# A folded layer's constant bias term: its own product replaced by two columns behind batch 1's x2

## The reference, cut to what matters

```python
x = x + L0(x, cond)      # base matrix + LoRA, summed over 8 experts
x = x + L1(x, cond)      # shared MLP + the 2 best of 8 experts' MLPs, 128 -> 512 -> 128
x = x + L2(x, cond)      # one expert of 8 (argmax of cond):
    # hidden = silu(x @ wu.T + bu) * (x @ wg.T + bg); out = hidden @ wd.T + bd
x = x + L3(x, cond)      # out = x @ (sum_g cond_g * weight_g * mask).T + bias
```

## Time and profile before

| | us |
|---|---|
| median of 3 runs | 72.28 |
| lowest and highest of them | 72.18, 72.62 |
| the profiled execution's own time | 72.77 |
| its span, first to last instruction | 71.5 |

### The profile page before, as it was taken

One profiled execution on the slowest core, in us unless ns is written; L12 is line 12 of the kernel. 1 busy time (PEld: TensorE's weight loads), 2 busy tenths in 40 slices (PEclk: granted clock), 3 DMA queues, 4 the chain that ended last, 5 costly groups with the idle time before them and its releaser, 6 DMA issues.

```text
span 71.5 us, 1059 instructions
## 1 busy us (share of the span) xinstructions
PE 68.1 (95%) x313; PEld 54.9 (77%) x313; DVE 45.2 (63%) x83; ACT 48.6 (68%) x97; POOL 36.7 (51%) x51
## 2 busy tenths in 40 slices
PE   5999999999999999999999999999999999999950
PEld 5976868778778778788788788787788788788640
DVE  0355669567655557765556775555986576958960
ACT  5225799466787666678766668869678895674660
POOL 5000478054999999866999986655540700000000
PEclk9999999999999999999999999999999999999998
DMA  0998799999500000000000000000000000000017
GB/s 3 240 339 286 288 392 375 409 413 416 218 5 9 0 0 0 0 0 0 0 5 5 0 0 0 0 0 9 0 0 0 0 0 0 0 0 0 0 40 253
DMA packets 2308, 6.62 MB, mean 93 GB/s; under 512 B 256, under 2 KB 768, under 8 KB 2304
## 3 DMA queue, kind: packets, MB, share of 16 engines
q1 hardware_dynamic: 2160, 6.44, 24.6%
q10 hardware_dynamic: 144, 0.13, 0.5%
HBM read 6.04 MB, written 0.52 MB: 92 GB/s over the span
## 4 chain that ended last, share of the span: by engine, by line
PE 95%; DVE 1%; issue 0%; DVEq 0%
PE gp L456 9%; PE gp L453 9%; PE gp L452 9%; PE acc L456 9%; PE acc L453 9%; PE acc L452 9%; PE up L456 9%; PE up L452 9%; PE up L453 9%; PE up L249 4%; PE acc L448 2%; PE acc L481 1%; PE up L607 1%; PE gp L448 1%; PE gp L438 1%; PE gp L568 1%
## 5 line engine op out<-in xcount | busy, mean ns | idle before, releaser
L379 ACT ACTIVATE act<-gp 128x512 f32<-128x512 f32 x24 | 14.3, 598 | 12.0 <-PE gp L456 11.5
L289 POOL TENSOR_TENSOR wlo<-raw_skill,whi 128x384 fp32r<-128x384 f32 x16 | 16.2, 1014 | 6.9 <-ACT whi L352 6.7
L671 DVE TENSOR_TENSOR hlo<-up,hhi 128x512 fp32r<-128x512 f32 x27 | 18.4, 682 | 1.9 <-ACT hhi L367 1.9
L664 DVE SCALAR_TENSOR_TENSOR up<-up,gate_w,act 128x512 f32<-128x512 f32 x16 | 12.1, 759 | 11.1 <-ACT act L379 11.0
L367 ACT ACTIVATE hhi<-up 128x512 fp32r<-128x512 f32 x27 | 16.1, 594 | 2.8 <-DVE up L657 2.6
L452 PE MATMUL acc<-hhi,whi 128*128 128x512 f32 (+1 forms) x28 | 11.2, 400 | 0.0
L452 PE MATMUL gp<-xhi,whi 128*128 128x512 f32 x27 | 11.1, 412 | 0.0
L456 PE MATMUL acc<-hlo,whi 128*128 128x512 f32 (+1 forms) x28 | 10.8, 387 | 0.0
L453 PE MATMUL acc<-hhi,wlo 128*128 128x512 f32 (+1 forms) x28 | 10.8, 386 | 0.0
L452 PE MATMUL up<-xhi,whi 128*128 128x512 f32 x27 | 10.7, 395 | 0.0
L456 PE MATMUL up<-xlo,whi 128*128 128x512 f32 x27 | 10.7, 395 | 0.0
(11 more groups left out here) (115 smaller groups left out, 94.2 us busy)
## 6 DMA issues: line engine op xcount, KB each, us to landing
raw_skill<-skill SPq DMA_DIRECT2D x4, 768.0 KB, 7.5
w3in<-l SPq DMA_DIRECT2D x1, 576.0 KB, 6.4
head_in<-head SPq DMA_DIRECT2D x2, 256.0 KB, 4.5
raw_l<-l SPq DMA_DIRECT2D x1, 386.5 KB, 8.5
raw_l<-l_folded SPq DMA_DIRECT2D x1, 386.5 KB, 8.4
head_in<-head SPq DMA_DIRECT2D x1, 384.0 KB, 4.2
head_in<-head SPq DMA_DIRECT2D x1, 321.0 KB, 3.1
out_t<-res SPq DMA_DIRECT2D x1, 256.0 KB, 2.1
```

What stands on the lines that cost most here:

```text
L289: pool.tensor_tensor(wlo[:, p, c], raw_piece(p)[:, c], whi[:, p, c], ALU.subtract).then_inc(s_wlo, 1)
L379: sc.activation(act[:, k % 2, :], gp[k % PAIRS][:, :], ACT.Gelu_apprx_tanh).then_inc(s_act, 1)
L664: ve.scalar_tensor_tensor(out=out, in0=u, scalar=gate_w[:, b, r:r + 1], in1=a, op0=ALU.mult, op1=ALU.mult).then_inc(s_h, 1)
L671: ve.tensor_tensor(hlo[:, i, t], hidden_of(k, t), hhi[:, i, t], ALU.subtract).then_inc(s_hlo, 1)
```

## The change

The one-column product of line 566 goes. In its place:

- `xhi` and `xlo` become views of tensors with two columns more (`xhi_bd`, `xlo_bd`), directly behind batch 1's x2. ScalarE copies the last two columns of `raw_l2` (the second gate bias and bd; the pair makes the width even) as their high part, right behind `w3hi`; VectorE makes their low part in the place where it added the bias.
- `l3_of_x2` takes 258 instead of 256 columns in the three passes of the second half, so that column 257 of `gp[1]` is W3 bd (`down3_bias`), counting from 0. It waits for the low part of the pair, and its last matmul releases `s_l3x2`.
- `bias31` is now made by ScalarE, with an Identity activation of the one column and the layer's bias, between `h_hi(26)` and `silu(27)`.
- TensorE waits for `bias31` no longer before `gate_up(23)`, but in `down_by_halves(26)` before its second half, which writes the bank that holds the column.
- ScalarE's splits of `down3` wait for two products instead of three.

```diff
-        xhi = sb("xhi", [P, 2, B, T], F32R)
-        xlo = sb("xlo", [P, 2, B, T], F32R)
+        xhi_bd = sb("xhi_bd", [P, 2 * B * T + 2], F32R)
+        xhi = xhi_bd[:, :2 * B * T].rearrange("p (l b t) -> p l b t", l=2, b=B)
+        xlo_bd = sb("xlo_bd", [P, 2 * B * T + 2], F32R)
+        xlo = xlo_bd[:, :2 * B * T].rearrange("p (l b t) -> p l b t", l=2, b=B)
...
-        down3_bias = down3_bank[:, L2_BLOCKS * P:L2_BLOCKS * P + 1]
+        down3_bias = gp[1][:, HALF + 1:HALF + 2]
...
+        bd = L2_BLOCKS * PIECE + 2 * L2_BLOCKS
+        bd_columns = raw_l2[:, 1, bd - 1:bd + 1]
...
                         sc.activation(w3hi[:, :], w3[:, 1, :], ACT.Copy).then_inc(s_w3hi, 1)
+                        sc.wait_ge(ld_l2[1], 16)
+                        sc.activation(xhi_bd[:, 2 * B * T:], bd_columns, ACT.Copy).then_inc(s_bdhi, 1)
                         for j in range(L2_BLOCKS):
-                            sc.wait_ge(s_down3, L2_BLOCKS + 1)
+                            sc.wait_ge(s_down3, L2_BLOCKS)
...
                 h_hi(N1 + 2)
+                sc.wait_ge(s_l3x2, 1)
+                sc.activation(bias31[:, :], down3_bias, ACT.Identity, bias=bias3).then_inc(s_bias31, 1)
                 silu(N1 + 3)
...
                         pe.wait_ge(s_down3lo, L2_BLOCKS)
-                        pe.wait_ge(s_bias31, 1)
...
                         t = slice(n * HALF, (n + 1) * HALF)
+                        if k == N1 + 2 and n:
+                            pe.wait_ge(s_bias31, 1)
...
-                    c = L2_BLOCKS * PIECE + 2 * L2_BLOCKS
-                    pe.matmul(down3_bias, w3[:, 1, :], raw_l2[:, 1, c:c + 1], start=True, stop=True).then_inc(s_down3, 1)
...
-                    for n in range(2):
-                        t = slice(n * HALF, (n + 1) * HALF)
-                        hi_passes(y1[n], w3hi[:, :], w3lo[:, :], xhi[:, 1, 1, t], True)
-                        lo_pass(y1[n], w3hi[:, :], xlo[:, 1, 1, t], False)
+                    pe.wait_ge(s_bdlo, 1)
+                    first = (2 * B - 1) * T
+                    for out, t in ((y1[0], slice(first, first + HALF)),
+                                   (gp[1][:, :HALF + 2], slice(first + HALF, first + T + 2))):
+                        hi_passes(out, w3hi[:, :], w3lo[:, :], xhi_bd[:, t], True)
+                        mm = lo_pass(out, w3hi[:, :], xlo_bd[:, t], True)
+                    mm.then_inc(s_l3x2, 1)
...
-                        ve.tensor_tensor(bias31[:, :], down3_bias, bias3, ALU.add).then_inc(s_bias31, 1)
+                        ve.wait_ge(s_bdhi, 1)
+                        ve.tensor_tensor(xlo_bd[:, 2 * B * T:], bd_columns, xhi_bd[:, 2 * B * T:], ALU.subtract)\
+                          .then_inc(s_bdlo, 1)
```

More of the change, by code:

```diff
@@ L208, in build @@
         s_down3lo = sem("s_down3lo")
+        s_bdhi = sem("s_bdhi")
+        s_bdlo = sem("s_bdlo")
+        s_l3x2 = sem("s_l3x2")
         s_bias31 = sem("s_bias31")
@@ L550, in down_by_halves @@
                         t = slice(n * HALF, (n + 1) * HALF)
+                        if k == N1 + 2 and n:
+                            pe.wait_ge(s_bias31, 1)
                         if k == N - 1:
                             pe.wait_ge(s_hhi, k + 1 + n)
-                        hi_passes(y1[n], whi[:, p, 2 * P:], wlo[:, p, 2 * P:], hhi[:, i, t], False)
+                        hi_passes(y1[n], whi[:, p, 2 * P:], wlo[:, p, 2 * P:], hhi[:, i, t], False, residual=True)
                         pe.wait_ge(s_hlo, k + 1 + (n if k == N - 1 else 0))
-                        mm = lo_pass(y1[n], whi[:, p, 2 * P:], hlo[:, i, t], is_last(k))
+                        mm = lo_pass(y1[n], whi[:, p, 2 * P:], hlo[:, i, t], is_last(k), residual=True)
                         if n or k == N - 1:
```

## The result

Measured together, with 19 runs of each, the changed kernel takes 71.81 us against 72.60 us for the kernel before (medians); the ratio is 0.9899, 95% interval 0.9875 to 0.9923. The medians lie 0.79 us apart, and the ratio makes it 1.01% or 0.73 us, where 0.22 us was forecast. The time itself is inside the range of 71.8 to 72.4, but at its very edge, and the step is over three times the one I had priced. The profiled execution took 71.99 us, with a span of 70.7 us.

What follows compares the result with a forecast made beforehand. TensorE, busy 95% of the span, was taken to bound the kernel. The product's -0.22 us and the six columns' +0.003 us made -0.22 us, so 72.28 us became 72.06 us, with a range of 71.8 to 72.4 us.

Steps and rivals of the forecast that it cites:

- The product: Fold, TensorE: removing line 566's two loads and two matmuls saves two weight-load steps of 0.11 us, 0.22 us.
- A: Fold: only the chain's share of the product goes, 0.12 us, giving 72.16 us; chance 0.10.
- B: Fold: loads are free and matmuls alone count, so 0.04 us goes, giving 72.24 us; chance 0.05.
- Six columns: `l3_of_x2`, second half: two more columns in each of three passes cost 3 ns.
- rival D: `l3_of_x2`, second half: 258-column passes lose the fast rate, 0.30 or 0.95 us more, 72.36 or 73.01 us; chance 0.04.
- ScalarE at the fold: Copy of 128x2 between lines 404 and 407, in ScalarE's idle time: costs nothing.
- the waits added to TensorE: In `l3_of_x2` and before the second half of `down_by_halves(26)`: met some 9 and over 1.6 us early, cost nothing.
- ScalarE before silu(27): New one-column activation after `h_hi(26)`, 0.29 us long, hidden by overlaps: cost 0, bounds 0 and 0.08 us.
- Rival C: Before silu(27): ScalarE's new instruction delays silu, giving back 0.08 us, 72.14 us; chance 0.08.
- The wider tensors: Addresses of tensors behind `xhi_bd` and `xlo_bd` shift by 8 or 16 bytes: costed at nothing.
- faster by over 1%: Whole kernel: a gain of over 1% (0.72 us) needs an effect that no step has; chance 0.02.
- The signs: 311 matmuls, line 568's load hidden, line 452's 0.22 us sooner, `l3_of_x2` passes 0.12 us, silu(27) awaiting TensorE, span 71.3.

Runs made afterwards that it cites:

- the wider tensors alone: Kernel before with `xhi` and `xlo` two columns wider, nothing else changed: ratio 0.9936, block 2.080 us.
- the first profile of the kernel before: Kernel before, unedited, as profiled for the prediction: the profiled execution took 72.77 us, block 2.100 us.
- the second profile of the kernel before: Kernel before run once more with no edit: ratio 0.9992, block 2.100 us.
- with `hlo` apart: Changed kernel with a 32-byte gap between `hhi` and `hlo`, moving `hlo` and all behind it: ratio 0.9959 to the kernel before, block 2.100 us.

## Why the prediction was right, and where it was not

- **The product, 0.22 us.** Right to the step: 2.766 to 2.546 us with nothing else changed. The loads' steps were the right reading, the chain's 0.12 us (A) and the 0.02 us between the two matmul records (B) the wrong ones. The 60 cycles (25 ns) for a small matmul, in the Trainium skill's page "TensorE: Matmul & The Clock Gate", section "Back-to-back issue gap", are its figure for a matmul by itself, and the section says that such figures are too small at few columns because the weight load is not in them. The trace agrees: each of the two matmuls cost 0.11 us.
- **Six columns, 3 ns.** 0.36 against 0.35 us for three passes, which the rows can't tell from 3 ns; rival D did not come.
- **ScalarE at the fold, VectorE's subtraction, the waits added to TensorE.** Hidden, as costed.
- **ScalarE before silu(27).** Hidden, with little to spare: the new instruction started 0.49 us after `h_hi(26)` (forecast 0.50) and lasted 0.26 us (forecast 0.29). Rival C did not come, but its premise, that a later silu reaches the end in full, was shown.
- **The wider tensors.** This is the term that was mis-sized. I wrote "I cost that at nothing, and no row prices it", and took the shift for 8 or 16 bytes where it was 32 and 64. It was worth 20 ns in each of the loop's blocks, 0.38 us over 19 of them and 0.47 us up to the end in the profile, and 0.46 us (0.64%) in the time: twice the product. For every other part the prediction gave a bound, a cover or a row of the same kind; zero here was a value with no reason behind it. The share of 0.02 for faster by over 1%, "an effect that no step has", was too small for the same reason: the result, 1.01%, lies right on that border.
- **The signs.** All of those for "right" came but one: the span, forecast at 71.3, was 70.7. It was a weak sign in any case: as the table from `down(0)` on shows, the start alone moves a span by over half a us.

That the time lies inside the range is luck. The forecast stood on a median of three runs, 72.28 us; with 19 runs the kernel before has 72.60. From 72.28, the measured step of 0.73 us leads to 71.55, outside the range. The starting value was 0.32 us too low and the step 0.5 us too small, and the two errors went against each other.

## What to carry to other kernels

An edit that resizes a tile moves everything allocated behind it, and in this kernel, which is bound by back-to-back matmuls, that alone moved the time by 0.64% (0.46 us), and another 32 bytes took it back. So compare the length of a loop block that the edit does not touch before crediting a gain to the edit, count from a row of the loop and not from the span's start, and measure the edit once more with padding that keeps all places as they were within a KB. In such a profile, price a small matmul by the steps between its weight loads, not by its share of the chain.

## What was not expected of the hardware

- The pace of float32r passes of 512 columns depends on where the tiles lie relative to each other: 2.100 us for nine passes (233.3 ns each) or 2.080 (231.1 ns), and values between, with the same instructions, no idle time and a mean granted clock of 0.996 to 1.000 in either case. Most layouts are steady, with 19 block lengths in a row of 2.080 us in the changed kernel's profile. Two of those between are not: with `hhi` and `hlo` moved by 64 bytes the blocks alternate between 2.093 and 2.100 us, and with the weights moved by 64 they go through four lengths from 2.085 to 2.100.
- In the changed kernel the 20 ns are not spread evenly. The steps from a pass of `up` by `xhi` and `whi` to the next are 226 ns, those of `acc` by `hhi` and `wlo` 236 ns, the same to 1 ns in two programs with the same layout (the wider tensors alone, and the change); in the first profile of the kernel before all kinds lie at 233 or 234. The block is the firmer measure, though: in the second profile of the kernel before single steps go from 230 to 237 ns, and with `hlo` apart the kinds lie between 230 and 237, both with blocks of 2.100.
- It is not the traffic of the DMA engines or of GpSimd that sets this pace. In the changed kernel, in these two stretches of 2.1 us the DMA engines move 413 GB/s and then none, GpSimd is busy for 0.46 and then 1.46 us, and the blocks in both take 2.080 us:

```profile
core 0: us, PE busy (x) PEld busy (x) DVE busy (x) ACT busy (x) POOL busy (x), PEclk, DMA share, GB/s
11.90:14.00 2.10, 2.10 (x11) 1.71 (x10) 1.41 (x3) 1.10 (x3) 0.46 (x3) 1.00 1.01 413
43.10:45.20 2.10, 2.10 (x11) 1.71 (x10) 1.35 (x2) 1.52 (x4) 1.46 (x3) 1.00 0.00 0
```

What causes it stays open. ScalarE and VectorE read and write in every block some of the tiles that were moved, so the runs don't tell whether TensorE's own reads set the pace or their meeting with those accesses: they show that the places matter, not how.
